# Attention and routed experts on one core: batch 0's nine-key products moved into the projection, absolute weight sums moved between the exponentials

## The reference, cut to what matters

```python
xn = layernorm(x)                                   # x: 4 batches x 1024 rows x 256
q = (xn @ Wq + bq) * D**-0.5;  k = xn @ Wk + bk;  v = xn @ Wv + bv     # 16 heads of D = 16
w = einsum('btd,bsd->bts', q, k)
w = w + rel_to_abs(einsum('btd,md->btm', q, rel_k))  # non-zero only for |s - t| <= 4: nine keys
p = softmax(w)
attn = (p @ v + rel_weights(p) @ rel_v) @ Wo + bo
logits = xn @ gate_w + gate_b                        # 8 experts, the 2 best per row
ffn = sum over the 2 chosen e of combine[t, e] * (silu(xn @ w1[e]) * (xn @ w3[e])) @ w2[e]
out = x + attn + ffn
```

## Time and profile before

| what | us |
|---|---|
| median of 3 runs (1893.63 to 1901.21) | 1894.43 |
| the profiled execution's own time | 1868.5 |
| its span | 1866.8 |
| TensorE busy | 1660.3 (89%) |
| VectorE busy | 1462.1 (78%) |
| ScalarE busy | 1097.4 (59%) |
| GpSimd busy | 758.6 (41%) |
| projection and routing end | 187.4 |
| first exponential of group 0 | 282.35 |
| last exponential of group 15 ends | 995.5 |

### The profile page before, as it was taken

The page is one execution under the profiler, slowest core; times in us unless marked ns, Lnnn a source line. Parts: engine busy times, 40 slices in busy tenths (PEclk is TensorE's granted clock), DMA queues, the critical chain, the costliest instruction groups (busy, mean ns, idle before and its releaser), DMA issues. The chain is left out here.

```text
span 1866.8 us, 35202 instructions
## 1 busy us (share of the span) xinstructions
PE 1660.3 (89%) x13691; PEld 1014.3 (54%) x13691; DVE 1462.1 (78%) x2633; ACT 1097.4 (59%) x2121; POOL 758.6 (41%) x535
## 2 busy tenths in 40 slices
PE   5995248999999999999994999999999999999991
PEld 3774002333333333333332788788887888878880
DVE  3556488888888899988822999989999899997652
ACT  3674005888888888888885554455544555445540
POOL 2000654555555555566100454445444454442120
PEclk9997557999999999999997999999999999999995
DMA  5997744784445545755204677777777777766745
GB/s 164 380 386 268 197 172 99 206 223 103 103 109 113 119 118 113 188 162 155 53 2 173 226 250 246 226 237 230 254 242 217 240 242 246 238 200 192 205 130 185
DMA packets 200806, 355.25 MB, mean 190 GB/s; under 512 B 17008, under 2 KB 147200, under 8 KB 192448
## 3 DMA queue, kind: packets, MB, share of 16 engines
q1 hardware_dynamic: 166240, 238.30, 43.1%
q0 software_dynamic: 25824, 93.73, 17.3%
q10 hardware_dynamic: 8576, 20.97, 2.9%
HBM read 281.47 MB, written 71.22 MB: 189 GB/s over the span
## 5 line engine op out<-in xcount | busy, mean ns | idle before, releaser
L855 DVE CUSTOM_DVE_ANT_0 t_seen<-t_s,hide 128x1024 bf16<-128x1024 f32 x512 | 610.9, 1221 | 82.3 <-PE t_s L714 81.6
L910 ACT ACTIVATE t_pr<-t_s 128x512 f32<-128x512 f32 x1024 | 559.1, 602 | 123.6 <-PE t_s L728 83.7
L714 PE MATMUL t_s<-t_ks,t_qs 48*128 48x512 f16 x1024 | 366.5, 406 | 79.1 <-DVE t_mx L855 55.6
L1436 ACT ACTIVATE e_sg<-e_pa,e_down 128x256 f32<-128x256 f32 x312 | 147.7, 473 | 397.1 <-PE e_pa L1311 392.3
L724 PE MATMUL t_s<-t_qs,t_ks 50*128 50x512 f16 x1024 | 350.0, 388 | 6.8 <-DMA t_qs<-t_mt 5.0
L1507 DVE SCALAR_TENSOR_TENSOR e_wl<-e_ws,e_up,e_wh 128x512 f16<-128x512 f32 x312 | 319.6, 1036 | 13.3
L741 PE MATMUL t_po<-t_pr,t_vx 128*32 128x256 f32 x4096 | 329.5, 394 | 0.1
L1320 PE MATMUL e_py<-e_w2s,e_hT 128*128 128x256 f32 x1248 | 322.9, 382 | 0.7 <-DVE e_hT L1529 0.7
L639 POOL TENSOR_TENSOR t_kw<-t_kw,t_qw 128x2304 f32<-128x2304 f32 x32 | 162.2, 5069 | 248.4 <-issue 180.9
L1311 PE MATMUL e_pa<-e_xh,e_wh 128*128 128x256 f16 x1248 | 239.8, 274 | 25.4 <-DVE e_xl L1499 18.5
L1248 POOL DMA_INDIRECT expert_sums<-e_y,e_token x78 | 140.5, 1801 | 291.7 <-DMA expert_sums<-e_y,e_token 204.8
(11 more groups left out here) (229 smaller groups left out, 1901.1 us busy)
## 6 DMA issues: line engine op xcount, KB each, us to landing
e_ws<-in_L_ffn_w_dram SPq DMA_DIRECT2D x78, 1024.0 KB, 5.3
e_w2s<-in_L_ffn_w_dram SPq DMA_DIRECT2D x39, 1024.0 KB, 6.4
e_vs<-v_rows POOLq DMA_DIRECT2D x32, 1152.0 KB, 6.0
t_kw<-k_rows POOLq DMA_DIRECT2D x22, 1152.0 KB, 9.7
a_wone<-in_L_ffn_w_dram ACTq DMA_DIRECT2D x16, 1024.0 KB, 8.9
t_qs<-q_parts SPq DMA_DIRECT2D x96, 128.0 KB, 4.1
t_ks<-k_parts SPq DMA_DIRECT2D x96, 128.0 KB, 8.0
t_kw<-k_rows SPq DMA_DIRECT2D x10, 1152.0 KB, 6.5
```

The costliest lines, as they stand in the source:

```text
L714: last = nc.tensor.matmul(s1[:, buf, half * CH:(half + 1) * CH], qs[lows, u, h, i * P:(i + 1) * P], ks[lows, u, h, half * CH:(half + 1) * ...
L855: nc.vector.tensor_tensor_reduce(out=seen[:, buf, :], in0=s1[:, buf, :], in1=c["hide"][:, (TB - 1 - i) * P:(TB - 1 - i) * P + L], scale=1. ...
L910: nc.scalar.activation(pr[:, k % BP, n % HG], s2[:, turn(u, n)], ACT.Exp, scale=SPREAD ** -2).then_inc(exp_ok, 1)
L1436: nc.scalar.activation(sg[:, f % 2, :], pa[:, f % PA, 0, :], ACT.Silu, scale=down[:, 0, bass.ds(s, 1)]).then_inc(g_ok, 1)
```

## The change

The q and k stacks of groups 0 and 1 get their memory before the projection and are loaded at the end of chunk 3 on SyncE's queue (18 DMAs of 128 KB). GpSimd makes batch 0's eight tiles of nine-key products, sums and additions to `band` during the projection, in `oa`, which is free then. Its nine constants for routing come behind that in its program. ScalarE no longer loads or sums weights in the projection. In the attention SyncE loads one weight matrix per group, and ScalarE sums its 2048 columns in four pieces of 512 behind exponentials 19, 28, 49 and 60 of the group; VectorE adds the pieces at the end. `channel_sums` leaves VectorE.

```diff
+def load_stack(eng, dr, stacks, g, u, row, came):
+    for dst, src, parts in ((stacks["qs"], dr["sq"], Q_PARTS), (stacks["ks"], dr["sk"], K_PARTS)):
...
+            eng.dma_start(dst[row + j * D:row + (j + 1) * D, u], src[g, part]).then_inc(came[u], 16)
...
# projection, SyncE, at the end of a chunk
+                    if n == 3:
+                        for p in range(PARTS):
+                            sp.wait_ge(st_part[p], 16 * 2 * KC * 2)
+                        load_stack(sp, dr, stacks, 0, 0, 0, stacks["in1"])
+                        load_stack(sp, dr, stacks, 0, 0, STACK, stacks["in2"])
+                        load_stack(sp, dr, stacks, 1, 1, 0, stacks["in1"])
...
# projection, GpSimd
+                def load(t):
+                    chunk = min((t + 1) * P + W - 1, T - 1) // CH
+                    pool.wait_ge(st_rows, 32 * (chunk + 1))
...
+                    load_window(pool, dr, t, qw[t % 2], kw[t % 2], win_in[t % 2])
+                def channel_sums(t):
...
+                    nc.gpsimd.tensor_tensor(held, held, q.rearrange("p (o e) -> p o e", o=1).broadcast_to([P, NM, E]),
+                                            ALU.mult).then_inc(sums_ok, 1)
...
+                    for f, w in enumerate((8, 4, 2)):
+                        pool.wait_ge(sums_ok, 5 * t + f + 1)
+                        nc.gpsimd.tensor_tensor(terms[:, :, 0:w], terms[:, :, 0:w], terms[:, :, w:2 * w],
+                                                ALU.add).then_inc(sums_ok, 1)
...
+                    if t + 2 < TB:
+                        pool.wait_ge(sums_ok, 5 * t + 5)
+                        load(t + 2)
+                def add_to_band(t):
...
+                    nc.gpsimd.tensor_tensor(scores, scores, dot[t % 2], ALU.add).then_inc(added_ok, 1)
+                load(0)
+                load(1)
+                for t in range(TB):
+                    after(pool, added_ok, t - 1)
+                    channel_sums(t)
+                    add_to_band(t)
...
# projection, ScalarE
-                    load_weights(n)
-                    sum_weights(n)
...
# attention, SyncE
+                def load_weights(i):
+                    after(sp, wpart_ok, 4 * i)
+                    sp.dma_start(wone[:], (w1, w3)[i // X][i % X].rearrange("(k p) f -> p k f", p=P)).then_inc(w_in, 16)
-                load1(0, 0)
-                load_window(sp, 0, 0, win_early)
-                load_window(sp, 1, 1, win_early)
-                load2(0, 0, 0, 0)
-                load1(1, 1)
-                for t in range(2, TB + 2):
-                    sp.wait_ge(part_ok, PIECES * (t - 1))
-                    load_window(sp, t, t % 2, win_early)
+                load_values(0, 0, 0)
+                load_weights(0)
...
+                    load_weights(g + 1)
# attention, GpSimd
-                products(0, 0, 0)
-                for t in range(TB):
...
+                for t in (TB, TB + 1):
+                    load_window(pool, dr, t, qw[:, t % 2, :], kw[:, t % 2, :], win_in[t % 2])
# attention, VectorE
-                        if g0 and n % HG > 0:
-                            channel_sums(n // HG, n // HG % 2, n % HG - 1)
-                        elif g0 and n // HG > 1:
-                            band_maximum(n // HG - 2)
+                        if g0 and n % HG == 1:
+                            band_maximum(n // HG)
...
+                dve.wait_ge(wpart_ok, 4 * 2 * X)
+                nc.vector.tensor_reduce(wsum[:], wpart[:], AX.X, ALU.add)
# attention, ScalarE
+                SUMS = (19, 28, 49, 60)
+                def sum_weights(i, piece):
+                    act.wait_ge(w_in, 16 * (i + 1))
+                    part = wone[:].rearrange("p k f -> p (k f)")[:, piece * CH:(piece + 1) * CH]
+                    nc.scalar.activation(part, part, ACT.Abs, accum_out=wpart[:, i, piece:piece + 1]).then_inc(wpart_ok, 1)
...
+                        if n in SUMS:
+                            sum_weights(g, SUMS.index(n))
```

More of the change, by code:

```diff
@@ L110, in norm_and_project @@
         most = sb("most", [P, 4])
-        wone = sb("wone", [P, 2, KC, F])
-        wsum_ok, wsum_in = sem("wsum_ok"), [sem(f"wsum_in{i}") for i in range(2)]
         logits = sb("logits", [P, NT, X])
@@ L204, in _ @@
                     sp.wait_ge(st_part[p], 16 * 2 * KC * NC)
+                for u in range(2):
+                    sp.wait_ge(stacks["in1"][u], 16 * 2 * len(Q_PARTS))
+                sp.wait_ge(stacks["in2"][0], 16 * 2 * len(Q_PARTS))
             @block.gpsimd
@@ L462, in norm_and_project, with attention @@
             route(nc, block, ctx, logits, rel_out, pT, dst, meta, spare, table, iota_e, slot_expert)
-def attention(nc, c, dr, band, bmax, neg, oa, dst, meta, spare):
+def attention(nc, c, dr, stacks, w1, w3, wsum, band, bmax, neg, oa, dst, meta, spare):
     XS = 2 * TB * HG
-    PIECES, FOLDS = 3, 4
+    FOLDS = 4
     MLEAD = 9
@@ L600, in step @@
                         load2(g + 2, b2, g2, u)
+                    else:
+                        sp.wait_ge(pv_ok, 2 * TB * (g + 1))
+                    load_weights(g + 1)
                 sp.wait_ge(s1_ok, X1)
```

108 lines of the change are left out of this document (53 added, 55 removed).

## The result

The changed kernel takes **1986.41 us** (median of 4 runs, 1975.26 to 1997.39) against 1894.03 for the kernel before on the same chip (4 runs, 1880.6 to 1901.21): a ratio of 1.055 [1.047, 1.063]. It is slower, and 94 us above the top of my range. The experiments ran in four sessions on different chips, and the kernel before had medians of 1893.0, 1930.7, 1891.4 and 1938.2 us in them, so times are compared by the ratio within a session. What a single edit does is therefore read from the trace's stage marks, one trace for each kernel.

What follows compares the result with a forecast made beforehand. PE was taken as the bound in projection and attention groups, the load-product-sum chain in group 0's first pass. -39.5 - 2.7 + 14.2 + 4.5 + 2 - 2 + 0.3 = -23.2 us: 1894.4 to 1871, range 1849 to 1892.

Steps and rivals of the forecast that it cites:

- Head of the attention: Group 0's lone first pass: without the load, product and sum chain, 39.5 us less, bounds 36 and 43.
- The weight load: Attention groups: the next weight matrix has from the third exponential to the 19th, 11 us, to load.
- the +2: Attention: cost of the weight-sum pieces on ACT, +2 us, with bounds 0 and 45 us.
- five places: Projection chunk: DVE must get in beside POOL at two L294 and three dependent steps of `normed`, together 7.1 us.
- 2.8 of it in excess: Projection: of 7.1 us a chunk of lock, 2.8 exceeds the slack; four chunks and a last L294 give +14.2 us.
- rival B: Projection: each place waits for a long POOL instruction as DVE and POOL fall into step; slower, bound 1943; chance 0.09.
- POOL's own end: Projection: POOL's products end at 173, then nine constants for routing; DVE gets there at 184, so this is hidden.
- The 18 stack loads: Projection, SP's queue after chunk 3: 7.6 us to issue, fitting into a chunk; cost 0, upper bound 5 us.
- -2.7: Projection: late last chunks take back 2.7 us once the weight loads, 2 MB a chunk, are gone.
- the 4.5 for the clock: Projection: PE's gaps lower its clock; one fall of some 9 us costs half of that, +4.5 us.
- Group 0's second pass: Attention: starting from a busier PE, part of its stretch at half clock may go, -2 us, bounds -8 and 0.
- rival C: Attention: half of the sums' 45 us on ACT comes onto PE's path with three banks; 1891, no difference; chance 0.13.

Runs made afterwards that it cites:

- the two-buffer kernel: The changed kernel with two weight buffers in the attention, each matrix loaded a group earlier into the other buffer: 1882.96 us, ratio 1.003.
- short pieces alone: The changed kernel with two weight buffers and POOL's work per batch 0 tile cut up (product in 9 instructions, folds in 6, 3 and 2): ratio 0.988.
- late stacks alone: The changed kernel with two weight buffers, long POOL instructions, and the 18 stack loads back at the start of the attention: ratio 0.995.
- the constants first: The changed kernel with two weight buffers, POOL's product in 9 instructions, stacks loaded at the attention's start, and routing's nine constants made before batch 0's first window: 1905.7 us, ratio 0.982.
- the early load: The changed kernel with one weight buffer, its load issued ahead of SP's wait for the group before and the loads behind that wait: 1871.81 us, ratio 0.999.
- the medium pieces: As the constants first, but with fewer, longer POOL pieces (product in 3 instructions, folds in 3, 2 and 1): 1902.77 us, ratio 0.985.
- the products alone: The changed kernel with the weight loads and sums back on ScalarE in the projection; batch 0's products stay on POOL there: 1889.6 us, ratio 1.007.
- the sums alone: The kernel before with only the weight sums moved into the attention, one buffer, batch 0's products left where they were: 2001.38 us, ratio 1.069.
- the short pieces with late stacks: The changed kernel with two weight buffers, POOL's product in 9 instructions, and the 18 stack loads at the attention's start: 1871.51 us, ratio 0.997.
- the sums with two buffers: The kernel before with only the weight sums moved into the attention, from two buffers loaded a group earlier: 1890.6 us, ratio 1.004.

## Why the prediction was wrong

Step by step, as it was put:

- **"Head of the attention: 39.5 us less."** Right: 40.1 to the first `t_mt`, in the stretch with the same clock.
- **"The weight load has from the third exponential to the 19th, 11 us."** This is the step that failed, and it alone carries the sign. It asked how long there was, and never put a duration of the load beside it. The load took 13.3 us, more than the 11 that I gave it. SP issued it some 12 us into the group (500.82, after the `t_mt` of 488.80): its wait ended with the fourth exponential, near the third that I had (497.66, 10.1 us before the first piece), but seven other DMAs took 3.2 of those, and what was left was 7 us. I costed the pieces on ACT with care (45 us of work, 0 to 45 as bounds) and they cost nothing, as the two-buffer kernel shows; the wait for their data cost 112 us. It wasn't in the +2, nor in its bounds, nor among the rivals. The kernel before's trace had a row for it, the same 1 MB loads in the projection:

```profile
L379 ACTq DMA_DIRECT2D a_wone<-in_L_ffn_w_dram x16: 374/452/1277, 31.1 to 152.4; - x16
...
DMA to landing us min/median/max: 4.9/8.9/12.2
```

  A median of 8.9 and a longest of 12.2 us, against 11 us, would have made this a rival with a price. And behind a wait of 8 us comes PE's clock: 9 us at 0.63.
- **"A chunk has five places ... L294, and three in the dependent steps of `normed`."** The mechanism was right and the place wrong. I had left out L253 (L330 after), whose only large input is one SBUF tensor; its four instructions took 8.8 us more than the 1.38 of before in each of two chunks, the most that any place lost.

```profile
L330 DVE TENSOR_SCALAR a_xn<-a_xt,a_mv,a_rstd x20: 401/639/5291, 71.3 to 170.5; 128x256 f32<-128x256 f32 x20
```

  Alone it takes 0.4 us; the longest took 5.29. The Trainium skill (SBUF — State Buffer, Who interferes with whom) does list tensor_scalar among the instructions that can run in a 2-port mode and then take the pair shared with GpSimd; I had used its rule on two inputs and passed over this one. The trace agrees that a tensor_scalar is held by GpSimd. It doesn't show that such a mode is the reason: alone, L253 takes 0.41 us, as long as L266, a tensor_tensor of the same 256 columns (0.41).
- **7.1 us a chunk of lock, 2.8 of it in excess.** Mis-sized. L330 and L371 alone lose 8.8 + 7.0 = 15.8 us in the chunk of 114 to 137. My mean over random arrivals was wrong in kind: after its first wait DVE isn't random any more. Each of the four L330 starts as POOL's last instruction ends and waits for POOL's next one, so they see the product and all three folds. I had this as rival B at 0.09, "because DVE and POOL fall into step", and the argument against it (the product is 40% of POOL's cycle) doesn't bear on it, since the folds count as well.
- **"POOL's own end ... so this is hidden."** Right as long as the lock made DVE later than POOL. Once the lock was gone it was a wait of 20.88 us.
- **The 18 stack loads, "I take 0, with 5 us as the upper bound".** Wrong once the lock is gone: 18.41 us for `a_xt`. With the lock they were nearly hidden (2.5 us, less than the 6.4 by which equal projections differ).
- **"-2.7" for the projection without the weights' loads and the 4.5 for the clock.** The -2.7 didn't come: with the weights' loads and sums gone and nothing put in their place the projection ended at 188.5 (two buffers) and 195.1, against 187.5. The clock fell to 0.70 in two windows of 17 us and to 0.80 in three others, more than the one stretch that I had.
- **"Group 0's second pass ... -2 us."** Not shown. From the first `t_mt` to the second it was 58.7 us before and 55.3 to 63.6 in the ten traces without the late load.
- **The 26 us between the profiled execution and the median** are for the most part explained below.

In sum the projection took +36.4 where I had +16. With the load in time that would have given my rival C's number, no difference, without C's mechanism. The 94 us above my range are the load and the clock behind it.

## What to carry to other kernels

When work is moved to an engine that has time for it, ask first when its data gets there: put the transfer's measured duration, beside the transfers it will share the engines with, against the time from its place on the issuing queue to the first use. Data that arrives late in an in-order queue stops everything behind it, and here one such stop of up to 8 us a group cost 112 us, more than twice the 45 us of work that was moved.

Holders hide one another. Here the shared way of DVE and POOL, the loads ahead of the hidden states and the constants behind the products lay on top of one another: short pieces alone gave 8.9 us and late stacks alone 2.5, the two together 10.2, and with the constants first all three gave 25.2 (219.7 to 194.5). When an edit that should give much gives little, look for the next wait at the same place before dropping the theory. If two engines lock each other out, cut the instructions of the one that has time, finely, and look in the trace whether the other gets in between the pieces; moving the one caught instruction away passed the wait to the next.

## What the hardware showed that I had not expected

**TensorE's clock falls while it is fully busy.** In the windows behind the last `t_mt`, of before and of after:

```profile
948.89:998.89 50.00, 47.46 (x485) 17.78 (x484) 0.00 (x0) 42.05 (x81) 0.20 (x1) 1.00 0.01 2
998.89:1048.89 50.00, 25.55 (x171) 20.35 (x171) 31.78 (x55) 22.04 (x36) 10.62 (x12) 0.76 0.76 265
```
```profile
1053.90:1103.90 50.00, 49.63 (x327) 13.93 (x327) 0.00 (x0) 33.64 (x67) 0.00 (x0) 0.62 0.07 22
1103.90:1153.90 50.00, 26.61 (x171) 9.69 (x170) 16.63 (x26) 22.86 (x34) 3.03 (x7) 0.53 0.39 141
```

The work is the same, the same code, far from the change. PE is busy throughout and gets 327 operations done in 50 us instead of 485, at a granted clock of 0.62. What it did just before the fall doesn't tell the two apart: in the first 10 us of the stretch it was busy 9.75 us with 107 operations in both, at full clock. The rest of the program behind the last `t_mt` took 917.9, 918.0, 918.6 and 919.0 us in the traces of before, of two buffers, of the early load and of the medium pieces; 941 to 943 in those of after, of the products alone, of both edits with the sums alone, of the short pieces with late stacks and of the constants first; and 928 in four others. So it comes in one execution or not, whatever the kernel, and is worth 24 us. That is probably most of the 26 us between the profiled 1868.5 and the median of 1894 which I couldn't explain: the profiled execution of before was one without it, and that the median one had it is inferred, since it has no trace. Its cause is open.

**The same in the projection.** With the sums alone moved, PE was busy 17.0 of 17 us and did less:

```profile
96.00:113.00 17.00, 17.00 (x64) 10.92 (x63) 7.64 (x34) 5.95 (x9) 0.00 (x0) 0.81 0.71 236
```

x64 against x89 to 90, at 0.81, with nothing on POOL. The same projection in the sums with two buffers did x91 in this window at 1.00. Their ends, 195.1 and 188.5, are 6.6 us apart, and the clock is the only difference that the windows show. In the sessions where the kernel before took 1930 and 1938 us, the traces have two groups of 67 to 79 us between 740 and 915 (clock 0.58 to 0.8), in all five kernels of those sessions. It was not tried whether the kernel before has them there too, since no trace of it was taken in those sessions.

**Full DMA engines at 60% of their rate.** The 18 stack loads kept the engines' share at 1.07 with 226 GB/s, where the projection's other traffic had 376 at 1.05. With short pieces the same window (113 to 130) moves 237 GB/s with the stack loads in it and 371 without them, both at full share. Which property of them does that was not measured by itself.
